# A gated block-sparse linear layer with LoRA: third row pair loaded transposed, row statistics broadcast through DRAM, new orders on all engines

## What is computed

```
xn = _layernorm(x)                                     # x: (2, 1024, 1024)
s  = einsum('bsk,nk->bsn', xn, masked(weight)) + bias
base   = einsum('bsi,oi->bso', xn, W_org)
scores = (mean(xn, axis=1) @ Wq.T) @ lora_keys.T / sqrt(128)
coeffs = softmax(scores)
h      = einsum('bsi,eir->bser', xn, lora_down)
delta  = einsum('be,bser,ero->bso', coeffs, h, lora_up)
out    = x + s * silu(base + delta)
```

## Time and profile before

| | |
|---|---|
| median of 3 runs | 440.56 us (438.39 to 443.45) |
| profiled execution | 440.17 us, span of the core 438.5 us |
| TensorE busy | 424.7 us, 97% of the span, 1910 matmuls |
| VectorE, ScalarE, GpSimd busy | 334.7, 216.4, 104.9 us |
| DMA | 101.05 MB, mean 230 GB/s |

### The profile page before, as it was taken

How to read it: one execution, slowest core, us unless ns; L and a number is a source line. 1 busy time by engine, 2 the same in 40 slices (tenths; PEclk the granted TensorE clock), 3 DMA queues, 4 the chain that set the end, 5 groups by cost and what they waited for, 6 DMA issues and landing times.

```text
span 438.5 us, 5903 instructions
## 1 busy us (share of the span) xinstructions
PE 424.7 (97%) x1910; PEld 345.7 (79%) x1910; DVE 334.7 (76%) x492; ACT 216.4 (49%) x379; POOL 104.9 (24%) x91
## 2 busy tenths in 40 slices
...
GB/s 299 413 416 240 161 266 255 280 210 218 195 237 264 265 290 283 290 325 362 179 73 144 49 114 275 287 236 336 410 386 165 96 76 21 72 270 242 265 160 96
DMA packets 40862, 101.05 MB, mean 230 GB/s; under 512 B 4608, under 2 KB 4864, under 8 KB 40064
## 3 DMA queue, kind: packets, MB, share of 16 engines
...
...
HBM read 71.31 MB, written 29.36 MB: 230 GB/s over the span
## 4 chain that ended last, share of the span: by engine, by line
PE 75%; DMA 14%; DVE 4%; POOL 2%; SPq 2%; issue 1%; ACT 1%; DVEq 0%; ACTq 0%; POOLq 0%
PE psA L864 24%; PE psA L866 24%; PE psA L865 24%; DMA x_nat_sb<-in_x_nat_dram 4%; DMA d_dram<-d_split 3%; DMA a_raw<-in_up_dram 2%; DMA out_dram<-cst 2%; DMA worg_sb<-in_w_org_dram 2%; DMA b_hi<-d_dram 2%; PE psA L883 1%; DVE nat_stats L1154 1%; DMA temp<-in_down_dram 1%; SPq L796 1%; DVE cst L1323 1%; POOL x_nat_sb L1365 1%
## 5 line engine op out<-in xcount | busy, mean ns | idle before, releaser
L864 PE MATMUL psA<-b_hi,a_hi 128*128 128x512 f32 (+1 forms) x444 | 173.6, 391 | 0.5 <-ACT snaps L1107 0.5
L866 PE MATMUL psA<-b_hi,a_lo 128*128 128x512 f32 (+1 forms) x444 | 172.1, 388 | 0.0
L865 PE MATMUL psA<-b_lo,a_hi 128*128 128x512 f32 (+1 forms) x444 | 172.0, 387 | 0.0
L864 PEld LDWEIGHTS psA<-b_hi,a_hi 128*128 128x128 f32 x444 | 83.4, 188 | 18.4 <-ACT snaps L1107 0.9
L866 PEld LDWEIGHTS psA<-b_hi,a_lo 128*128 128x128 f32 x444 | 83.4, 188 | 17.1
L865 PEld LDWEIGHTS psA<-b_lo,a_hi 128*128 128x128 f32 x444 | 83.4, 188 | 16.6
L1078 ACT ACTIVATE b_hi<-b_raw 128x512 fp32r<-128x512 f32 (+2 forms) x66 | 45.3, 716 | 56.0 <-DVE b_raw L1232 36.5
L1219 DVE TENSOR_TENSOR b_lo<-b_raw,b_hi 128x512 fp32r<-128x512 f32 (+2 forms) x66 | 52.0, 814 | 8.6 <-ACT b_hi L1078 8.3
L1395 POOL TENSOR_TENSOR cst<-cst,xres 128x512 f32<-128x512 f32 x15 | 23.0, 1534 | 98.7 <-DVE cst L1323 98.7
L1107 ACT ACTIVATE snaps<-psA 128x512 f32<-128x512 f32 x39 | 23.2, 595 | 42.8 <-PE psA L866 42.6
L1219 DVE TENSOR_TENSOR a_lo<-s_raw,a_hi 128x512 fp32r<-128x512 f32 x52 | 37.4, 733 | 5.2 <-ACT a_hi L1068 5.2
...
## 6 DMA issues: line engine op xcount, KB each, us to landing
xn_dram<-xq SPq DMA_DIRECT2D x16, 512.0 KB, 5.8
...
xq<-xn_dram SPq DMA_DIRECT2D x16, 512.0 KB, 5.5
...
x_nat_sb<-in_x_nat_dram SPq DMA_DIRECT2D x14, 512.0 KB, 5.0
```

The source lines that it names most:

```text
L864: nc.tensor.matmul(ps, l_hi, r_hi, start=first, stop=False, skip_group_check=True)
L865: nc.tensor.matmul(ps, l_hi, r_lo, start=False, stop=False, skip_group_check=True)
L866: return nc.tensor.matmul(ps, l_lo, r_hi, start=False, stop=over, skip_group_check=True)
```

## The change

- Pair 2 (tiles 4 and 5) is no longer transposed on TensorE: it is loaded transposed and normalised in place by N4 and N5, as the later pairs are (`BY_ROWS = 2` takes the place of `WFIRST` there). Pair 2 keeps its 8 plain products.
- Mean and scale of tiles 4 to 15 go through DRAM: BS t stores `stat` (128 x 2 numbers) to `stat_dram`, BL t loads it with a broadcast to all 128 partitions into `bc`, whose layout is now interleaved. BA, BP and BC are gone. Both new steps are in SP's order.
- Tile 1's statistics are made on ScalarE (XS1, X1), its scale on GpSimd (XR1).
- Six of the 16 sums R are made on ScalarE (R5, R6, R9, R10, R11, R15), eight instructions each.
- lora_down loads alternate between two buffers (`temp[:, 2 + k % 2]`).
- All five texts of `ORDER` are new. What TensorE multiplies, and in which order, is the same from P4 on but for the place of the two small G products.

```diff
-    CP0 TX0.0 TX0.1 P0 K CP1 TX1.0 TX1.1 P1 TX2.0 TX2.1 P2 TX3.0 P3 TX3.1 CP2 P4 P5 CP3 P6 TX4.0 TX4.1 P7 P8 P9
-    P10 TX5.0 P11 P12 TX5.1 P13 P14 BP6 P15 P16 P17 BP7 BP8 P18 P19 P20 BP9 P21 P22 P23 P24 P25 P26 BP10 P27 P28
...
+    CP0 TX0.1 TX0.0 P0 TX1.0 TX2.0 TX1.1 CP1 P1 TX2.1 TX3.0 P2 TX3.1 P3 K CP2 P4 P5 CP3 P6 P7 P8 P9 P10 P11 P12
...
+        bc, _ = at("bc", [P, 2, P, 2], F32, r2_at + H * 4)
...
+                elif kind == "BS":
+                    t = st[1]
+                    sp.wait_ge(pool_rstd, rstd_num[(t,)] + 1)
+                    sp.dma_start(stat_dram[t], stat[:, t % 2, :]).then_inc(stat_stored[t % 2], 16)
+                elif kind == "BL":
+                    t = st[1]
+                    sp.wait_ge(stat_stored[t % 2], 16 * stat_count(t))
+                    if (t - 2,) in n_num:
+                        wait_rows(sp, t - 2)
+                    row = stat_dram[t].rearrange("(o r) s -> o (r s)", o=1)
+                    sp.dma_start(bc[:, t % 2, :, :].rearrange("p r s -> p (r s)"), row.to_broadcast([P, 2 * P]))\
+                      .then_inc(bc_loaded[t % 2], 16)
...
-                    sp.dma_start(temp[:, 3, :], down_t[k]).then_inc(d_loaded, 16)
+                    sp.dma_start(temp[:, 2 + k % 2, :], down_t[k]).then_inc(d_loaded[k % 2], 16)
...
+                elif kind == "R":
                     t = st[1]
...
+                    wait_rows(act, t)
+                    for k in range(KC):
+                        n = act_r_num[(t,)] * KC + k
+                        if n >= 4:
+                            act.wait_ge(act_R, n - 3)
+                        nc.scalar.activation(row_copy[:, n % 4, :], x_tile(t // 2, t % 2)[:, k * P:(k + 1) * P], ACT.Copy,
+                                             accum_out=xpart[:, t, k:k + 1]).then_inc(act_R, 1)
```

More of the change, by code:

```diff
@@ L140 @@
-    HB2.4.1 HB2.2.3 HB2.2.2 H83 QS87 H81 HB2.6.1 H86 HB2.5.2 HB2.5.3 HB2.4.2 H87 HB2.4.3 HB2.6.2 HB2.6.3 H88 QS90
-    QS91 H90 QS92 QF92 H85 QF93 H84 QO94 QF88 H93 QS96 H92 H95 QS98 H89 QS99 H91 QF95 H96 QF98 H94 QO100 H100
-    QF101 QF102 QS103 H101 H98 H97 QS105 QF105 QS106 QO107 H102 H99 QF108 QS109 QS111 QF111 QF112 QO113 TF0 TF1
-    """,
-    """
-    SN0 CA0.1 CB0 CM0 W0.0 W0.2 W0.1 VB0.0.0 VB0.0.2 VB0.0.1 W0.3 V4 SN1 CB1 R0 KD CM1 SN2 R1 SN3 W1.1 V0 V2 CA3.1
-    CB2 VB0.0.3 CB3 VB0.1.1 V1 VB0.1.0 V5 CM2 QC2 V3 SN5 SN4 V6 CM3 LN5 R3 VB0.7.0 W3.0 V7 QC6 V8 VB0.2.0 QC7 QC3
@@ L167 @@
-    QM111 QC112 QR111 QM112 QM113 TQ0 TQ1 TM0 TM1 TR0 TR1
-    """,
-    """
-    SR0 LN0 SR1 LN1 W1.0 SR2 LN2 SR3 LN3 W2.0 SR5 SR4 LN4 XR6 XR8 T0.0.2 XR7 XR9 XR10 S3.1 S3.3 XR11 XR12 XR13
-    XR14 XR15 S4.4 S5.3 S6.3 S6.1 S6.4 S7.1 S7.2 S8.3 S8.4 T1.1.1 S9.1 T1.3.1 T1.0.3 T1.1.3 T1.1.2 QR64 QR74 S11.4
-    S12.3 S12.1 QR73 S12.2 QR77 QR80 S12.4 QR84 QR83 T2.1.1 S13.3 T2.3.1 T2.0.3 T2.1.2 S13.2 S14.3 S14.1 QR92
-    S14.4 QR98 QR100 QR101 QR105 QR108 QR112 QR113
+    LX0 LM0 LX1 LW0.0 LW0.1 LX2 LX3 LM1 LM2 LW1.0 LY LM3 LW1.1 LX4 LI LW2.0 LK LW3.0 RS0 LX5 RS2 RS1 LX6 LT6 BS4
@@ new lines @@
+    P92 P93 P94 P95 P96 P97 P98 P99 P100 P101 P102 P103 P104 P105 P106 P107 P108 P109 P110 P111 P112 P113 P114
+    """,
+    """
+    CA0.1 XS1 TC0.0 X1 H4 HB0.0.3 TC0.1 CA1.0 CA1.1 TC1.0 H0 TC1.1 H6 HB0.0.0 HB0.0.2 TC2.0 CA3.1 H2 HB0.1.0 TC2.1
+    H5 H1 H3 HB0.0.1 TC3.0 HB0.1.1 X4 TC3.1 X5 HB0.7.0 X6 H7 HB0.2.0 X7 X8 H8 X9 HB0.5.0 H10 H11 X10 H9 X11 PB3.0
+    R5 HB0.4.0 X13 H13 X12 HB0.6.0 H12 HB0.3.0 X14 R6 H14 QS24 H20 H15 H16 H18 PB3.1 PB4.1 QS26 H17 X15 PB4.0 QS28
+    H19 R9 H25 H22 H21 QS29 H23 D0 H26 QO30 QS33 H24 R10 PB5.0 H32 QS35 H31 H27 QS36 PB5.1 H29 H28 QO37 H30 D1 H34
@@ new lines @@
+    QF101 H98 H93 QF95 QS103 H101 QO100 H97 H100 QS105 H102 QF105 QF102 QS106 H99 QS109 QO107 QF108 QS111 QF111
+    QF112 QO113 TF0 TF1
+    """,
+    """
+    SN0 CA0.0 CB0 CM0 W0.0 W0.1 W0.3 SN2 R0 SN3 V4 CB1 CA2.1 V0 CM1 CA2.0 CA3.0 W1.1 V2 CB2 V6 VB0.0.3 VB0.0.2 V1
+    VB0.1.0 VB0.0.1 CB3 V5 VB0.0.0 V3 VB0.1.1 CM2 R3 QC2 KD QC3 R2 R1 CM3 W3.0 VB0.7.0 QC6 N4 V7 R4 VB0.2.0 T0.0.3
+    N5 QC7 V8 T0.0.1 T0.0.2 QC13 V9 QC12 V10 QC14 V11 T0.0.4 N6 QC15 VB0.5.0 VB0.4.0 N8 V12 N7 V13 QC22 R8 QC19
```

234 lines of the change are left out of this document (118 added, 116 removed).

## The result

The changed kernel takes 464.6 us (median of 4 runs, 459.4 to 466.2) where the kernel before takes 439.6 in the same session: a ratio of 1.054, 95% interval 1.049 to 1.059. It is slower by some 24 us; the prediction said 434.3 us, 430 to 440. Some executions of this study ran in a slower state; they count in the medians in us but not in the ratios, so the two can differ, most of all in e16, where it was two of four.

What follows compares the result with a forecast made beforehand. TensorE's own work was taken as the bound, busy 424.7 of 438.5 us. From the profiled 440.17: -4.6 (transposes) - 3.1 (waits) + 0.3 (start) + 0.5 (VectorE, trip) + 1.0 (ScalarE) gave 434.3 us, range 430 to 440.

Steps and rivals of the forecast that it cites:

- Part 1: TensorE: the transposes of tiles 4 and 5 and of BP go, saving 4.6 us; the term held surest.
- Part 3: Start, up to P4: P4 begins near 34.3, 0.3 us later than before; bounds -3 and +2 us.
- Part 2: TensorE's three later waits, for W_org's addition, lora_down's reload and a ScalarE copy, go: 3.1 us saved.
- I take all three as gone: TensorE's later waits of 1.7, 0.9 and 0.5 us all counted as removed, minus the allowance in Part 5.
- clock at the start: Rival: low clock lasts 4 us longer at the start, costing 2 us; P4 at 36.3, total 436.3; chance 0.10.
- Part 4: VectorE's order and the statistics' trip through DRAM: 0.5 us of new waiting, bounds 0 and 2.
- Two make 10, N4 begins at 49.0, and nothing waits: Tile 4's statistics: store and load at 5.0 us each, ready before N4's limit of 49.5; no wait.
- 24 more DMAs on SP lie beside everything: SP's queue: the added DMAs, at about 0.4 us each, run beside other work and got no price.
- Part 5: ScalarE gains six R at 3.6 us each; 1.0 us allowed for lateness and new-order waits, bounds 0 and 5.
- the 0.5 us allowed: New waiting of P8 for VB0.7.0, forecast to end at 45.3 with P8 due at 45.4.
- Late trip: Rival: tile 4's store and load take 15.5 us each, N4 begins at 70, total 454.8; chance 0.06.
- the two rivals near 436.3: Only the transposes count (436.4, chance 0.17) and the start's low clock (436.3, chance 0.10), on the border of "faster".

Runs made afterwards that it cites:

- e16: e2's kernel with the twelve small statistics stores back and nobody waiting for their landing; 450.9 us, ratio 1.016 to the kernel before.
- e2: e1's kernel without the statistics stores; BL loads part of an input row and waits for no store; 440.2 us, ratio 1.000 to the kernel before.
- e11: e2's kernel with LU0.3 and DS7 moved ahead of LG9.1, RS14 and LG10.0 in SyncE's order; 439.7 us, ratio 0.998 to the kernel before.
- e4: Changed kernel with the six R of ScalarE put back on VectorE; 463.4 us, ratio 1.049 to the kernel before.
- e7: e1's kernel with N4 and R4 moved behind VB0.2.0 in VectorE's order; 455.7 us, ratio 1.035 to the kernel before.
- e1: Changed kernel with a stat slot for every tile, X t waiting for tile t - 2's power, not its store; 453.1 us, ratio 1.028 to the kernel before.

## Why the prediction was wrong

**Part 1, the transposes, 4.6 us.** Right in mechanism: e2, which has only these left, is busy 421.7 against 424.7, with some 14 slow matmuls (2.8 us behind E0 and E1 together) in it, so 5.8 us less without them. Counted in the two timelines, 1.1 of these lie ahead of P4, which is Part 3, and 4.7 behind it, where the 4.6 were forecast.

**Part 2, three waits, 3.1 us.** The causes named were the right ones: taken alone, the two buffers give 1.2 us (0.9 predicted; the interval takes in nothing) and QR83 2.9 (1.7 predicted, the end of its interval). "I take all three as gone" failed as a sum: in the changed kernel's orders E0 and E1 have new last waits (2.5 and 2.2 us, plus the low clock behind them), and e2 and e11 show such waits of 2.0 to 2.8 us without any store. The gain went there.

**Part 3, the start.** P4 began at 33.5 for 34.3, so this part held. The rival "clock at the start" did not come in the profiled execution, whose clock is full from 9 to 73 us. But it is not ruled out: the profiles of e4, e7 and e16, whose TensorE has the same order there, have P4 in time and then a granted clock of 0.50 from 34 or 35 us on for 3.4 us, with no wait over 0.6 us since 20 us. That is 7 matmuls at 0.43 us, 1.4 us in all, where the rival had 2.

**Part 4, the trip. The step that failed.** In the words of the prediction, three terms are at fault. "Two make 10, N4 begins at 49.0, and nothing waits": two trips took 12.9 us, N4 began at 51.0, the bound of 49.5 was right, and P12 waited 1.8 us. That is small, and e7 shows that removing the stall behind it gains nothing. "24 more DMAs on SP lie beside everything": they don't. BL's wait at the head of the queue, N's wait behind it, BS's wait for GpSimd and the slowed traffic cost 12 us (e16, e2); the text named the first and gave it no price. And the largest single term, 11.7 us (e1), was not in the text at all: the text priced BS and BL by who *reads* the result, and overlooked who must wait to *overwrite* the source. X t was released before by a copy on ScalarE itself, two tiles earlier; now it is released by a landing. The line stood in the change (L1054). The Trainium skill's rule on pieces under 512 B ("DMA: Bandwidth & Descriptors", Specifications) was quoted and given no price, as an estimated 4 us for the two legs looked harmless; the store's landing alone took 7.3 us in the median here.

**Part 5, ScalarE.** R took 8 x 0.30 us pipelined with its readings, 2.4 us in the timeline, not 3.6, and e4 shows no difference that is clear of noise from where R stands (1.049 against 1.054, the intervals overlap). The bounds held. VB0.7.0 ended at 44.1, and P8 did not wait for it: the 0.5 us allowed weren't needed.

**The rivals.** "Late trip" had the right place and sign and 0.06 of the chances. Its 454.8 us, from a single stall of 20.5 us, is not what happened: the stalls were many and at most 4.6 us. Its price was worked out for one tile's trip at the start, where it is nearly harmless, and not for twelve of them in a row. Its argument against ("after 40 us SP issues little") counted issues and not bytes: the DMA share there is 0.84. The chances also don't add up as worded: half of the two rivals near 436.3 is 0.14, where the sum for "faster" has 0.06. The range of 430 to 440 had no room for a mechanism outside the five parts.

**Clock.** No part priced what the clock adds behind a later stall. Most stalls of 2.0 to 6.9 us in these traces are followed by 5 to 13 matmuls at 1.2 GHz, which is 1.0 to 2.6 us more for each stall; in the changed kernel it was 7.0 us over four stalls. In the kernel before the longest later stall is 1.7 us and the clock stays full.
